# Wider moving operands in the first and third product of a three-product attention kernel

## What is computed

```python
Wh = X @ W.T                                # 8192 x 256
s_i = Wh @ r_src; s_j = Wh @ r_dst
e = s_i[:, None] + s_j[None, :]             # 8192 x 8192
e = jnp.where(e >= 0, e, ALPHA * e)         # ALPHA = 0.2
e = jnp.where(A == 0, -jnp.inf, e)          # A: 0/1 matrix, 8192 x 8192 int32
attention = jax.nn.softmax(e, axis=1)
h = jax.nn.gelu(attention @ Wh, approximate=False)
out = _layernorm(x + h, axis=-1)
```

## Time and profile before

| what | value |
|---|---|
| median of 2 runs | 1663.07 us (1662.44 and 1663.69) |
| span of the profiled execution | 1658.4 us |
| PE busy / PEld busy | 1572.9 us (95%) / 1548.5 us (93%) |
| DVE busy | 1528.0 us (92%) |
| ACT busy | 1177.3 us (71%) |
| POOL busy | 435.6 us (26%) |
| mean granted TensorE clock | 0.983 |
| DMA | 164.36 MB, mean 99 GB/s |

### The profile page before, as it was taken

The page is one execution under the profiler, slowest core; times in us unless marked ns, Lnnn a source line. Parts: engine busy times, 40 slices in busy tenths (PEclk is TensorE's granted clock), DMA queues, the critical chain, the costliest instruction groups (busy, mean ns, idle before and its releaser), DMA issues.

```text
span 1658.4 us, 37778 instructions
## 1 busy us (share of the span) xinstructions
PE 1572.9 (95%) x12685; PEld 1548.5 (93%) x12685; DVE 1528.0 (92%) x1916; ACT 1177.3 (71%) x1527; POOL 435.6 (26%) x615
## 2 busy tenths in 40 slices
PE   5869999999999999999999999999999999999996
PEld 3659999999999999999999999999999999999996
DVE  2669999999999999999999999999999999999996
ACT  2556777777776777777676776777677777767773
POOL 1002223223232321323232223232332132323221
PEclk9999999999999999999999999999999999999998
DMA  6237766877667685867677686867768686776751
GB/s 106 98 80 104 102 84 90 127 93 120 90 93 111 92 122 76 128 82 111 98 107 103 81 128 82 127 85 106 108 92 126 80 127 83 99 110 96 106 77 38
DMA packets 296416, 164.36 MB, mean 99 GB/s; under 512 B 11440, under 2 KB 290224, under 8 KB 296368
## 3 DMA queue, kind: packets, MB, share of 16 engines
q0 software_dynamic: 270336, 134.25, 62.3%
q1 hardware_dynamic: 26032, 29.67, 5.8%
HBM read 289.67 MB, written 8.42 MB: 180 GB/s over the span
## 4 chain that ended last, share of the span: by engine, by line
PE 81%; DMA 6%; issue 6%; DVE 3%; ACT 3%; POOL 0%; SPq 0%; DVEq 0%; POOLq 0%; ACTq 0%
PE acc L650 27%; PE acc L660 27%; PE acc L653 27%; DMA Pw<-in_x 6%; DVE Pw L509 3%; ACT P_hi L420 2%; PE acc L608 0%; DVE P_lo L519 0%; ACT gates L347 0%; SPq L189 0%; DMA R_row<-w_rows 0%; DMA w_rows<-w_in 0%; DVEq L509 0%; POOL adj_in L250 0%; PE acc L619 0%
## 5 line engine op out<-in xcount | busy, mean ns | idle before, releaser
L650 PE MATMUL acc<-WV_hi,P_hi 128*128 (+1 forms) x4096 | 1009.2, 284 | 37.8 <-ACT P_hi L420 37.8
L653 PE MATMUL acc<-WV_lo,P_hi 128*128 (+1 forms) x4096 | 1006.8, 283 | 0.0
L650 PEld LDWEIGHTS acc<-WV_hi,P_hi 128*128 128x128 f32 x4096 | 781.2, 191 | 42.1 <-issue 30.4
L420 ACT CAST P_hi<-Pw 128x1024 fp32r<-128x1024 f32 x512 | 536.0, 1047 | 370.4 <-DVE Pw L509 213.9
L653 PEld LDWEIGHTS acc<-WV_lo,P_hi 128*128 128x128 f32 x4096 | 779.5, 190 | 0.0
L509 DVE SCALAR_TENSOR_TENSOR Pw<-R_row,X,gatesT 128x512 f32<-128x512 f32 x1024 | 748.1, 782 | 2.5 <-DMA R_row<-w_rows 2.5
L519 DVE TENSOR_TENSOR P_lo<-Pw,P_hi 128x1024 fp32r<-128x1024 f32 x512 | 626.7, 1224 | 50.9 <-ACT P_hi L420 48.6
L660 PE MATMUL acc<-WV_hi,P_lo 128*128 (+1 forms) x4096 | 581.4, 285 | 0.8 <-DVE P_lo L519 0.8
L250 POOL DMA_DIRECT2D adj_in<-in_adj x512 | 329.2, 650 | 903.6 <-ACT gates L347 889.9
L347 ACT ACTIVATE gates<-adj_in 128x1024 uint8<-128x1024 bf16 x512 | 536.8, 1048 | 33.3 <-DMA adj_in<-in_adj 24.9
L660 PEld LDWEIGHTS acc<-WV_hi,P_lo 128*128 128x128 f32 x4096 | 533.2, 191 | 1.0 <-DVE P_lo L519 1.0
(11 more groups left out here) (58 smaller groups left out, 264.1 us busy)
## 6 DMA issues: line engine op xcount, KB each, us to landing
adj_in<-in_adj POOLq DMA_DIRECT2D x512, 256.0 KB, 5.3
Pw<-in_x SPq DMA_DIRECT2D x32, 256.0 KB
x_res<-in_x SPq DMA_DIRECT2D x64, 128.0 KB, 2.3
out<-y SPq DMA_DIRECT2D x64, 128.0 KB, 6.0
R_row<-w_rows SPq DMA_DIRECT2D x16, 256.0 KB, 6.8
w_in<-in_L_gnn_W SPq DMA_DIRECT2D x1, 256.0 KB, 2.7
w_rows<-w_in SPq DMA_DIRECT2D x1, 32.0 KB, 2.1
r_in<-in_L_gnn_r SPq DMA_DIRECT2D x1, 2.0 KB, 2.7
```

Of the source, the lines that this page charges most:

```text
L420: nc.scalar.copy(P_hi[:, u % 2], Pw[u][:]).then_inc(s_hi, 1)
L650: nc.tensor.matmul(acc[r_][:, v, 0:HC], P_hi[:, u % 2, par, bass.ts(v, P)], WV_hi[:, k, :], start=(first and u == 0 and par == 0), stop=False)
L653: nc.tensor.matmul(acc[r_][:, v, 0:FOUT], P_hi[:, u % 2, par, bass.ts(v, P)], WV_lo[:, k, :], start=False, stop=False)
```

## The change

The first product reads 320 columns in place of 258, the third 280 in place of 258. WV_hi is viewed as one flat row in each partition, so the further columns are the start of the next slice's row. They are added into columns 258 to 319 (or 279) of the same PSUM bank, which nothing reads. In the last group of a block the products of the second slice keep 258 columns, since behind the last row of WV_hi there is nothing to read. The second product is as before, with 256 columns.

```diff
+        WV_flat = WV_hi[:].rearrange("p k f -> p (k f)")
...
                 def piece(ah, r_, c, first=False, final=False):
+                    def wide(u, par, columns):
+                        return HC if final and u == GP - 1 and par == 1 else columns
+
...
                             for v in range(RT):
-                                nc.tensor.matmul(acc[r_][:, v, 0:HC], P_hi[:, u % 2, par, bass.ts(v, P)],
-                                                 WV_hi[:, k, :], start=(first and u == 0 and par == 0),
-                                                 stop=False)
+                                nc.tensor.matmul(acc[r_][:, v, 0:wide(u, par, 320)], P_hi[:, u % 2, par, bass.ts(v, P)],
+                                                 WV_flat[:, bass.ds(HC * k, wide(u, par, 320))],
+                                                 start=(first and u == 0 and par == 0), stop=False)
                                 nc.tensor.matmul(acc[r_][:, v, 0:FOUT], P_hi[:, u % 2, par, bass.ts(v, P)],
                                                  WV_lo[:, k, :], start=False, stop=False)
...
                             for v in range(RT):
-                                last = nc.tensor.matmul(acc[r_][:, v, 0:HC], P_lo[:, u % 2, par, bass.ts(v, P)],
-                                                        WV_hi[:, k, :], start=False,
+                                last = nc.tensor.matmul(acc[r_][:, v, 0:wide(u, par, 280)], P_lo[:, u % 2, par, bass.ts(v, P)],
+                                                        WV_flat[:, bass.ds(HC * k, wide(u, par, 280))], start=False,
                                                         stop=(final and u == GP - 1 and par == 1))
```

## The result

The changed kernel takes **1777.3 us** (median of 2 runs, 1776.97 and 1777.63) against 1663.07: a ratio of 1.0685, interval 1.0665 to 1.0705. It is 114 us slower. 1740 was forecast, with a range from 1710 to 1800. The span of the profiled execution grew by 117.6 us, 3.4 more than the median. In every run whose time and span are both on record the time is 1.6 to 1.8 us above the span (here 1777.63 and 1776.0). So of the 4.0 and 5.3 us between the span and the two timed runs of before, only 1.6 to 1.8 are the start and the end around the instructions; for the rest, the profiled execution was itself some 3 us shorter than the timed ones.

The account below looks back on a forecast made before the run. PE, at one matmul per 119 ns, was taken to bound the kernel. Span 1658.4 + 81 (columns) - 5 (waits) + 1 (clock) = 1735 us; with 4.7 us from span to median, 1740, range 1710 to 1800.

Parts of the forecast that it names:

- The bound: Main stage: PE sets the pace, with 81% of the chain that ended last, so whatever a matmul costs more is paid.
- The second chain: PE at full clock: weight loads of 112 to 119 ns beside a 107 ns stream, so the first 11 ns are free.
- a surcharge on top: PE at full clock: the 11 ns beyond the stream add to it, so no widening is free; upper bound +141 us.
- the sign of the surcharge: First and second product as a pair: 265 ns or more would show that every column is paid; 253 to 258 expected.
- First product: 4032 matmuls widened from 258 to 320 columns: +18 ns each, at least +15.3, upper bound +25.8.
- Third product: 4032 matmuls widened from 258 to 280 columns: +2 ns each, upper bound +9.2.
- Second product: 256 columns behind a wide matmul: the distance stays 119 ns, so 0 change.
- The waits: PE's waits in piece 4, behind POOL's addition: 16 get shorter by some 0.3 us, -5 us (upper-bound case -8).
- The lower clock: Stretches at 0.50 in ten blocks stay: +1 us; -15 if they vanish, up to +9 if all 16 blocks have one.
- all columns are paid: Rival for PE's matmuls: load and stream disturb each other, every further column costs; 1796 us; 1760 to 1805 at 0.30.
- the load chain: Main forecast for PE's matmuls: loads beside the stream hide the first widening; 1715 to 1760 us at 0.48.
- The queue: Rival: loads and matmuls fetched ahead let wide ones borrow from narrow ones; +11 us, 1674; 1650 to 1696 at 0.12.

## Why the prediction was right, and which step of it failed

**The bound** was read rightly: PE sets the pace, what a matmul costs more is paid, and no other engine took over.

**The second chain** failed. I held that loads of 112 to 119 ns lie beside a stream of 107, so that the first 11 ns of widening are free: "A second chain beside the stream". Both parts of the change run alone, and 512 columns, show the other case that I had put beside it, a surcharge on top: already the first 22 further columns cost 0.43 ns each. The pair of first and second product takes 265 ns, which the prediction had named as the sign of the surcharge. The evidence for the chain was the earlier trace rows, from the matmuls just behind an idle time, and the prediction named that as its weak point. Its other support, 165 ns at the lower clock, doesn't fit the kernel with fewer columns, where the loads start 213 ns apart. A chain of loads may be there, but not one of 112 to 119 ns at the full clock that hides columns.

**First product:** +18 ns was forecast with an upper bound of 25.8; 27.7 came, over the bound by the small share that each further column costs beyond its cycle. **Third product:** +2 was forecast with a bound of 9.2; 9.3 to 9.5 came. **Second product:** 0 was right, within 1 ns. The sum was 81 us with 62 and 141 as bounds, and is 146, over the upper one.

**The waits** fell by 15 us where 5 (or 8) were forecast. That they shrink with a slower PE was right, the size was not: a group became 8 x 37 = 296 ns longer and the wait shorter by 0.99 us, from 1.98 to 0.99; with the first product alone 222 ns and 0.66 us, with the third alone 75 ns and 0.27 us. That is three groups' worth or more each time, where I had taken two.

**The lower clock** was taken to stay (+1 us), with -15 as the other end. It went. (With all 16 blocks disturbed the prediction's own terms give 16 x 1.6 - 15 = +11, not +9; nothing hangs on it.) The step that failed is "The PE would still idle some 1.6 us in each block, so I leave them". It failed twice: PE idles 1.0 us, not 1.6, and even the waits of 1.7 us with the third product alone had a fall behind one of 14 only. Of the single waits in these kernels, the clock fell behind 10 of 13 of 1.92 to 2.04 us (258 columns), 1 of 14 of 1.67 to 1.72 us (280 in the third), none of 14 of 1.26 to 1.33 us (320 in the first) and none of 14 of 0.96 to 1.00 us (both). With 258 columns and all waits at 1.34 us or less (the shortened, split and later additions) there was no fall either. The step is not sharp, though: with added DVE work pairs of 0.55 or 0.75 and 1.2 us had a fall behind them twice. So waits of 1.3 us or less are enough to end the falls, without a further column. Whether the columns do something too is not shown: in the kernels with 280 and 320 the idle time changed together with them.

So the forecast of 1740 was short by 65 us in the columns, and long by 26 in clock and waits. That the two errors go against each other is luck, and that the time lies in the range owes much to the range, which was wide enough for the rival too. The measured 1777 lies in the stretch given to the rival "all columns are paid" (1760 to 1805, at 0.30), not in that of the load chain (1715 to 1760, at 0.48). The rival, at 1796, was the right mechanism, and 19 us too high, mostly for the clock and the waits. **The queue** did not even anything out: at the full clock the distance behind a matmul is that of its own columns, and behind the second product it stays at 118 ns, beside 258, 320 or 512 columns. **The Trainium skill**, in "TensorE: Matmul & The Clock Gate", section "Back-to-back issue gap", has columns over 2.4 plus 2.5 ns. This case agrees with it for bf16 (110.7 and 110.3 ns measured at 258 columns, where the rule gives 110.0; 109.3 at 256, where it gives 109.2) and not for fp32r (119.4). Its sustained 131 ns for 512 columns isn't seen here: fp32r took 230.

## What to carry to other kernels

Before padding an operand to fill what looks like free time in a matmul's distance, take one product to another width and look at the distance behind it; matmuls just behind an idle time do not stand for the steady stream. What a short engine operation costs when it blocks another depends on its place: here the same addition, of the same length, cost 48 us in one place and 18 in another (1613.87 us without it, 1632.24 with it later). Look at what the blocked engine would have done for whom, and move the operation by one wait, which here gave 1.9% while the whole widening lost 6.9%. If a wait brings a lower clock behind it, shorten the wait rather than feed the array columns that nobody reads.

## What the runs showed that I had not expected

- fp32r matmuls cost some 12 ns more than their columns at 2.4 GHz (119.4 ns at 258) and nothing more at 1.2 GHz (427 ns at 512, 267 at 320); bf16 ones cost some 3 ns more (110.7 ns), and plain f32 ones 2 ns over twice their columns (217 ns).
- With fp32r matmuls of 192, 128 and 64 columns the granted clock stayed at 0.50 throughout a main stage without idle time, and the weight loads started 213 ns apart whatever the width: half the columns made the kernel 66% slower (2759.6 us).
- Four POOL operations of no use made a kernel 11 us faster by delaying the one behind them.
